# Moving the lower part of x to GpSimd and keeping the normalised x in PSUM

## The chip, the cores and the metric

One core of a Trainium2 chip. A core has TensorE (PE, matrix products, with a weight-load half PEld), VectorE (DVE), ScalarE (ACT), GpSimd (POOL) and SyncE (SP, which issues the transfers here). They run side by side and wait for each other through semaphores; matrix products land in PSUM, which has eight banks of 512 fp32 columns; all else is in SBUF. The metric is device time in microseconds of one execution, the median over runs.

## The reference

The input x is 16 sequences of 128 tokens with 128 features. It goes through one gated cross-attention, and then through six layers of local attention and feed-forward:

```python
x = x + tanh(g_xattn) * xattn(layernorm(x), ctx)
h = layernorm(x)
for i in range(6):
    h = attn_layer(shift_tokens(h), Wqkv[i], ...) + h   # 16 heads, windows of 32, rotary, l2norm
    h = ffn_layer(shift_tokens(h), g[i], b[i], W1[i], ...) + h
x = x + tanh(g_ffn) * h
```

`ffn_layer` normalises its input by feature, xn = (x - mean) / sqrt(var + 1e-5) * g + b, multiplies it by W1 (128 x 682), gates one half with the gelu of the other, and multiplies by W2.

## The kernel before

After a prologue for the cross-attention (some 75 us) the kernel runs 6 layers x 8 pairs of sequences = 48 pairs through a software pipeline. Each engine has its own loop over pairs with a body `step`, written out by hand, in which each call names its lag: `chunk(1, 0, 0)` on PE is product 1 of this turn's pair, sequence 0; `up(1, 2)` belongs to the pair of two turns before. The order of the calls is the order of the engine's queue, so an instruction that waits holds up all that follow it on its engine. GpSimd's loop is one turn behind the others: its `lag` of 1 or 2 stands for the pair that DVE calls with 0 or 1.

Products that need more precision than one pass split their operands in an upper and a lower part: x into `xsh` (ACT, `x_parts`, L538) and `xsl` = x - `xsh` (DVE, `x_rest`, L780), and the weights likewise into `Wh` and `Wl` (GpSimd, L384). A `product` is three matmuls, L1003 to L1005. The first product of a turn is `chunk(1, 0, 0)`, the second `chunk(0, 0, 0)`. Each waits for `xs_split` (xsl is there) and then for those who empty its bank: the first for earlier readers of a chunk, the second for ACT's copy `v_out(0, 1, 1)` (L576).

The normalisation for the feed-forward goes: PE `centre` puts the centred x into bank 3, ACT `deviations` squares it, PE `variance` averages, ACT `inverse_deviation` makes `rstdx` (L608, L611), DVE `normal` makes `xng` = centred x * g * `rstdx` in SBUF (L841), ACT `upper_x` adds b and rounds to `xfh` (L618), DVE `lower_x` makes `xfl` = xng + b - xfh (L849), and PE's `up` multiplies both parts by W1.

GpSimd adds the two halves of the rotary (`add`, L393), multiplies by the inverse norms (`normalise`, L407), divides by row sums (`divide`, L413) and makes `Wl`. Bank order is a table, `BANK_USERS`; `FREED` names who releases a bank after each kind of use. Bank 3's user after "xc" is `v_chunk(0, 0, 0)`.

Of the kernel before, what the change touches and what calls it, by code (L numbers as in the profile page):

```python
# [5 lines left out]
L, NB, S, D = 6, 16, 128, 128  # L6
# [25 lines left out]
def program(nc, x, ctxT, Wqkv, Wo, W1, W2, by_feature, every_token, shape_consts, out):  # L32
# [5 lines left out]
    def sb(name, shape, dt=F32):  # L38
        return es.enter_context(nc.sbuf_tensor(name, shape, dt))
# [4 lines left out]
    with es:  # L44
# [16 lines left out]
        F_LNG = 2 * 128 + 3  # L61
# [29 lines left out]
        sqx = sb("sqx", [128, 2 * S])  # L91
        lvx = sb("lvx", [128, 2 * S])
        rstdx = sb("rstdx", [128, 2 * S])
        xng = sb("xng", [128, 2 * S])
        xfh = sb("xfh", [128, 2 * S], F32R)
        xfl = sb("xfl", [128, 2 * S], F32R)
        gate = sb("gate", [128, KT2, 2 * S])
# [31 lines left out]
        def sems(name, n):  # L129
# [12 lines left out]
        res_done, xs_split, xng_done, xf_ready, hh_ready, h_ready = (  # L142
            sem(s) for s in ("res_done", "xs_split", "xng_done", "xf_ready", "hh_ready", "h_ready"))
        DVE_SEMS = (rot_done + ss_done + t2_done + mx_done + sc_out + sum_done + rs_done
                    + [res_done, xs_split, xng_done, xf_ready, hh_ready, h_ready])

        sq_done, v_ready, q_ready, k_ready = sems("sq_done", 4), sems("v_ready", 2), sems("q_ready", 2), sems("k_ready", 2)
        exp_done, PT_ready, OT_ready = sems("exp_done", 2), sems("PT_ready", 2), sems("OT_ready", 2)
# [5 lines left out]

        add_done, qk_ready, P_ready = sems("add_done", 4), sems("qk_ready", 4), sems("P_ready", 2)
        ss_ready, W_split = sem("ss_ready"), sem("W_split")
        POOL_SEMS = add_done + qk_ready + P_ready + [ss_ready, W_split]

        x_read = (ch_full[2], v_full[0])
        xf_read = up_full[2]  # L160
# [12 lines left out]
        def n_(n):  # L173
            return n + START

        def pipeline(eng, step, split_lag=0):
# [11 lines left out]
            for it in range(PAIRS, PAIRS + LAST):  # L188
# [7 lines left out]
                 "turn_p": lambda k: [PT_ready[k]],  # L196
                 "values": lambda k: [OT_ready[k]],
                 "Wo": lambda k: [res_done],
                 "xc": lambda k: [xng_done],
                 "up": lambda k: [[gelu_done], [hh_ready], [hh_ready]][k],  # L200
                 "down": lambda k: [h_ready]}
        BANK_USERS = [
# [47 lines left out]
        def column(at, pair, per=1, k=0, rows=slice(0, 128)):  # L250
            return fc[rows, ds(pair // LAYER_PAIRS * per + (at + k), 1)]
# [6 lines left out]

        def halves_of_pair(pair):
            return [R[64 * g:64 * g + 64, ds(pair % LAYER_PAIRS * 2, 2), g:g + S] for g in range(2)]  # L260

        def two(ap):
            return ap.rearrange("p (r s) -> p r s", r=2)
# [111 lines left out]
        @block.gpsimd  # L375
        def _(pool):
            for s in POOL_SEMS:
                pool.sem_inc(s, START)

            def lower_part(k, block):  # L380

                pool.wait_ge(high_ready, k + 1 + START)
                pool.sem_inc(wait_met, 1)
                nc.gpsimd.tensor_tensor(part_block(Wl, k, block), raw_block(block), part_block(Wh, k, block),  # L384
                                        ALU.subtract).then_inc(W_split, 1)

            def step(it, on, splitting):

                def add(c, lag, r):
                    n = (it - lag) * 2 + r  # L390
                    pool.wait_ge(rot_done[c], n_(n) + 1)
                    pool.wait_ge(t2_done[c], n_(n) + 1)
                    nc.gpsimd.tensor_tensor(u[:, r, c], u[:, r, c], t2[:, r, c % 2], ALU.add).then_inc(add_done[c], 1)  # L393

                def bound_norms(lag, r):
                    n = (it - lag) * 2 + r
                    for c in range(NCH):
                        pool.wait_ge(ss_done[c], n_(n) + 1)
                    pool.wait_ge(ln_done, n_(n) - 1)
                    pool.sem_inc(wait_met, 1)  # L400
                    nc.gpsimd.tensor_scalar_max(ssc[:, r], ss[:, r], 1e-24).then_inc(ss_ready, 1)

                def normalise(c, lag, r):
                    n = (it - lag) * 2 + r
                    pool.wait_ge(rn_ready, n_(n) + 1)
                    pool.wait_ge(add_done[c], n_(n) + 1)
                    nc.gpsimd.tensor_tensor(by_head(u[:, r, c]), by_head(u[:, r, c]),  # L407
                                            spread(rn[:, r, HC * c:HC * c + HC], HC, DH), ALU.mult).then_inc(qk_ready[c], 1)

                def divide(e, lag, r):  # L410
                    n = (it - lag) * 2 + r
                    pool.wait_ge(rs_done[e], n_(n) + 1)
                    nc.gpsimd.tensor_tensor(P[:, r, e], P[:, r, e], spread(rs[:, r, e], 8, DH),  # L413
                                            ALU.mult).then_inc(P_ready[e], 1)

                def split_low():
                    pair = it - LOW_LAG
                    lower_part(pair + LAYER_PAIRS, pair % LAYER_PAIRS)

                if on(2):  # L420
                    normalise(0, 2, 1)
                    add(2, 2, 1)
                    add(1, 2, 1)
                    normalise(2, 2, 1)
                    normalise(1, 2, 1)
                    divide(0, 2, 0)
                    divide(1, 2, 0)
                if on(1):
                    add(1, 1, 0)
                    add(0, 1, 0)  # L430
                if splitting:
                    split_low()
                if on(2):
                    divide(1, 2, 1)
                    divide(0, 2, 1)
                if on(1):
                    add(2, 1, 0)
                    bound_norms(1, 0)
                    normalise(2, 1, 0)
                    normalise(1, 1, 0)  # L440
                    add(3, 1, 0)
                    normalise(0, 1, 0)
                    normalise(3, 1, 0)
                    add(3, 1, 1)
                    bound_norms(1, 1)
                    add(0, 1, 1)
                    normalise(3, 1, 1)

            pool.wait_ge(in_ready, 16 * N_INPUTS)
            pool.sem_inc(c_ctx, START)  # L450
            with pool.Fori(0, NB // PAIR) as pair:
                pool.wait_ge(rest_ready, pair * 32 + START)
                for j in range(2):
                    g = pair * 2 + j
                    pool.wait_ge(c_v, g - 1 + START)
                    pool.sem_inc(wait_met, 1)
                    nc.gpsimd.tensor_copy(cT[j], ctxS[:, ds(g * GB, GB)].rearrange("p b d -> p (b d)")).then_inc(c_ctx, 1)
                for i in range(4):
                    lower_part(pair * 4 + i, pair * 4 + i)

            for w in range(2):
                nc.gpsimd.tensor_tensor(TC[:, :, w], qs[:, w], rc[:, w].unsqueeze(1).broadcast_to([128, L, DH]), ALU.mult)
                for a in range(2):
                    o, i = 32 * a, 32 * (1 - a)
                    nc.gpsimd.tensor_tensor(TS[:, :, w, o:o + 32], qs[:, w, :, i:i + 32],
                                            rsn[:, w, o:o + 32].unsqueeze(1).broadcast_to([128, L, 32]),
                                            ALU.mult).then_inc(tables_ready, 1)
            pool.wait_ge(tables_ready, 4)
            pipeline(pool, step, LOW_LAG)

        @block.scalar
        def _(act):
# [57 lines left out]
            def step(it, on, splitting):  # L530
# [82 lines left out]
                def upper_x(lag):  # L613
                    pair = it - lag
                    act.wait_ge(xng_done, n_(pair) + 1)
                    act.wait_ge(xf_read, n_(pair))
                    act.sem_inc(wait_met, 1)
                    nc.scalar.activation(xfh[:], xng[:], ACT.Identity, bias=column(F_LNB, pair)).then_inc(xfh_done, 1)  # L618

                def gelu(lag):  # L620
                    pair = it - lag
# [83 lines left out]
        def _(dve):  # L705
# [67 lines left out]

            def step(it, on, splitting):

                def x_rest(lag):
                    pair = it - lag
                    dve.wait_ge(xsh_ready, n_(pair) + 1)
                    dve.sem_inc(wait_met, 1)
                    nc.vector.tensor_tensor(xsl[:], shifted_pair(pair), xsh[:], ALU.subtract).then_inc(xs_split, 1)  # L780

                def squares(c, lag, r):
                    n = (it - lag) * 2 + r
                    dve.wait_ge(sq_done[c], n_(n) + 1)
# [51 lines left out]
                def normal(lag):  # L836
                    pair = it - lag
                    dve.wait_ge(rstd_ready, n_(pair) + 1)
                    dve.wait_ge(xfh_done, n_(pair))
                    dve.sem_inc(wait_met, 1)  # L840
                    nc.vector.scalar_tensor_tensor(out=xng[:], in0=bank_of("xc")[:, 0:2 * S], scalar=column(F_LNG, pair),  # L841
                                                   in1=rstdx[:], op0=ALU.mult, op1=ALU.mult).then_inc(xng_done, 1)

                def lower_x(lag):
                    pair = it - lag
                    dve.wait_ge(xfh_done, n_(pair) + 1)
                    dve.wait_ge(xng_done, n_(pair) + 1)
                    dve.sem_inc(wait_met, 1)
                    nc.vector.scalar_tensor_tensor(out=xfl[:], in0=xng[:], scalar=column(F_LNB, pair), in1=xfh[:],  # L849
                                                   op0=ALU.add, op1=ALU.subtract).then_inc(xf_ready, 1)  # L850

                def gated(lag):
# [25 lines left out]
                if on(1):  # L878
                    straight(2, 1, 1)
                    swapped(1, 1, 1)  # L880
                    swapped(2, 1, 1)
                if on(0):
                    x_rest(0)
                if on(2):
                    normal(2)
                if on(1):
# [387 lines left out]
```

## Time and profile before

| | |
|---|---|
| median of 3 runs | 1595.66 us (1594.83 to 1598.72) |
| profiled execution, its time / its span | 1600.49 / 1598.6 us |
| busy, share of the span | PE 94%, PEld 78%, DVE 88%, ACT 74%, POOL 73% |
| mean granted PE clock | 0.976 of full |
| xsl L780 on DVE | 48 x 1341 ns mean |
| xng L841 / xfl L849 on DVE | 48 x 472 / 917 ns mean |
| xfh L618 on ACT | 48 x 510 ns mean |

A row of the time line has the start (us from the span's start), the busy time of the group in us, engine, line, operation, the tiles written and read, and the count; in brackets the engine's idle time before it and who ended it. A row of the table of waits has the waiting engine and line, whom it waited for, and the total, the number and the longest of these waits in us.

### The profile page before, as it was taken

The page shows a single profiled execution, that of the slowest core. Times are in us where ns is not written, and L with a number is a line of the kernel's source. Part 1 is how long each engine was busy: PE and PEld are TensorE (multiplying, and loading weights), DVE is VectorE, ACT ScalarE, POOL GpSimd, SP SyncE. Part 2 cuts the span into 40 slices and gives each one's busy share as a digit, 9 for nine tenths or more (in the row PEclk, how much of TensorE's full clock was granted, in tenths as well). Part 3 has the DMA queues.
Part 4 walks back from the last instruction along what each step waited for, and adds up shares of the span by engine and source line. Part 5 has one row for each costly group of instructions (what it writes and reads, how often), then busy time and mean ns, then how long its engine had stood idle before and what let it go on. Part 6 is the DMA issues. An engine that isn't in the chain of part 4 may idle for free.

```text
span 1598.6 us, 80227 instructions
## 1 busy us (share of the span) xinstructions
PE 1506.6 (94%) x31136; PEld 1251.0 (78%) x31136; DVE 1399.6 (88%) x2545; ACT 1175.3 (74%) x2333; POOL 1168.4 (73%) x1118
## 2 busy tenths in 40 slices
PE   4589999999999999999999999999999999999996
PEld 3367888888888888888888888888888888888875
DVE  3587899999999999989999999999999999999982
ACT  3456687788778778778877877877877777777772
POOL 1276777878877887787787788788778777777760
PEclk8689999999999999999999999999999999999996
DMA  5110011011110111101112110111110101000010
GB/s 144 42 44 28 28 36 42 26 49 58 31 36 26 42 39 57 41 26 36 42 29 68 29 38 29 33 42 61 36 35 20 30 25 62 29 20 30 20 30 28
DMA packets 41462, 62.40 MB, mean 39 GB/s; under 512 B 3662, under 2 KB 30412, under 8 KB 41420
## 3 DMA queue, kind: packets, MB, share of 16 engines
q1 hardware_dynamic: 41420, 61.84, 13.2%
q8 instruction: 27, 0.44, 0.1%
q14 instruction: 15, 0.12, 0.0%
HBM read 18.84 MB, written 1.05 MB: 12 GB/s over the span
## 4 chain that ended last, share of the span: by engine, by line
PE 86%; issue 4%; ACT 3%; DVE 2%; ACTq 1%; POOL 0%; DVEq 0%; POOLq 0%
PE bank L1010 13%; PE bank L1080 12%; PE bank L1092 10%; PE bank L1003 9%; PE bank L1053 8%; PE bank L1004 8%; PE bank L1005 8%; PE bank L1127 5%; PE bank L1116 3%; PE bank L1035 3%; PE bank L1117 2%; PE bank L1118 2%; ACT v L576 2%; DVE xng L841 1%; PE bank L1106 1%
## 5 line engine op out<-in xcount | busy, mean ns | idle before, releaser
L393 POOL TENSOR_TENSOR u<-u,t 128x512 f32<-128x512 f32 x384 | 498.2, 1308 | 40.5 <-DVE t L802 40.5
L407 POOL TENSOR_TENSOR u<-u,rn 128x512 f32<-128x512 f32 x384 | 401.8, 1068 | 78.8 <-ACT rn L556 78.8
L413 POOL TENSOR_TENSOR P<-P,rs 128x512 f32<-128x512 f32 x192 | 196.5, 1045 | 172.6 <-DVE rs L826 172.6
L1003 PE MATMUL bank<-Wl,xsh 128*128 (+1 forms) x576 | 273.4, 475 | 26.1 <-ACT v L576 22.7
L802 DVE TENSOR_TENSOR t<-bank,TS 128x512 f32<-128x512 f32 x384 | 258.0, 682 | 28.1 <-ACT sq L545 25.5
L793 DVE TENSOR_TENSOR u<-bank,TC 128x512 f32<-128x512 f32 x384 | 261.9, 682 | 6.0 <-ACT sq L545 3.1
L786 DVE TENSOR_REDUCE ss<-sq 128x8 f32<-128x512 f32 x384 | 250.5, 673 | 6.4 <-ACT sq L545 6.4
L1004 PE MATMUL bank<-Wh,xsl 128*128 (+1 forms) x576 | 228.5, 397 | 0.0
L1005 PE MATMUL bank<-Wh,xsh 128*128 (+1 forms) x576 | 228.0, 396 | 0.0
L545 ACT ACTIVATE sq<-bank 128x512 f32<-128x512 f32 x384 | 218.9, 598 | 5.8 <-PE bank L1005 5.3
L1010 PE MATMUL bank<-shape_constants,u 128*128 128x128 f32 x1536 | 219.2, 275 | 3.4 <-POOL u L407 3.2
L1010 PEld LDWEIGHTS bank<-shape_constants,u 128*128 128x128 f32 x1536 | 182.2, 141 | 34.9 <-POOL u L407 5.0
L562 ACT COPY qT<-bank 128x512 f32<-128x512 f32 x192 | 115.2, 600 | 122.3 <-PE bank L1010 121.1
L1080 PEld LDWEIGHTS bank<-PT,vs 64*64 64x64 f32 x6144 | 163.9, 135 | 37.5 <-issue 37.5
L1080 PE MATMUL bank<-PT,vs 64*64 64x32 f32 x6144 | 187.8, 220 | 3.0 <-ACT PT L588 3.0
L1080 PE MATMUL bank<-PT,v 64*64 64x32 f32 x6144 | 186.1, 219 | 2.6 <-issue 2.6
L1092 PE MATMUL bank<-OT,WoS 128*128 128x256 f32 x768 | 175.5, 382 | 1.2 <-ACT OT L594 1.2
L1080 PEld LDWEIGHTS bank<-PT,v 64*64 64x64 f32 x6144 | 164.7, 135 | 2.8 <-issue 2.8
L1003 PEld LDWEIGHTS bank<-Wl,xsh 128*128 128x128 f32 x576 | 109.5, 190 | 62.5 <-issue 55.7
L1092 PEld LDWEIGHTS bank<-OT,WoS 128*128 128x128 f32 x768 | 143.4, 192 | 19.2 <-issue 1.3
L1053 PEld LDWEIGHTS bank<-kT,qT 64*32 64x32 f32 x12288 | 123.3, 105 | 32.3 <-issue 32.3
L594 ACT COPY OT<-bank 128x512 f32<-128x512 f32 x192 | 109.1, 594 | 45.4 <-PE bank L1080 45.4
(102 smaller groups left out, 3040.0 us busy)
## 6 DMA issues: line engine op xcount, KB each, us to landing
vs<-v SPq DMA_DIRECT2D x96, 384.0 KB, 3.3
Wraw<-in_L_ffn_Wqkv_dram SPq DMA_DIRECT2D x72, 117.5 KB, 2.1
WoS<-in_L_ffn_Wo_dram SPq DMA_DIRECT2D x6, 512.0 KB, 3.7
W1h<-Wh SPq DMA_DIRECT2D x6, 341.0 KB, 2.5
W1l<-Wl SPq DMA_DIRECT2D x6, 341.0 KB, 2.9
Wraw<-in_L_ffn_W_dram SPq DMA_DIRECT2D x12, 116.0 KB, 2.2
OT<-in_x_dram SPq DMA_DIRECT2D x2, 512.0 KB, 5.6
v<-in_ctx_dram SPq DMA_DIRECT2D x2, 512.0 KB, 6.9
```

The costliest lines, as they stand in the source:

```text
L393: nc.gpsimd.tensor_tensor(u[:, r, c], u[:, r, c], t2[:, r, c % 2], ALU.add).then_inc(add_done[c], 1)
L407: nc.gpsimd.tensor_tensor(by_head(u[:, r, c]), by_head(u[:, r, c]), spread(rn[:, r, HC * c:HC * c + HC], HC, DH), ALU.mult).then_inc(qk_re ...
L786: nc.vector.tensor_reduce(ss[:, r, HC * c:HC * c + HC], by_head(square_out(c, r)), AX, ALU.add).then_inc(ss_done[c], 1)
L793: nc.vector.tensor_tensor(by_head(u[:, r, c]), by_head(bank_of("chunk", c, r)[:]), TC[:, layer(it - lag), c % 2].broadcast_to([128, HC, DH ...
L802: nc.vector.tensor_tensor(halves(t2[:, r, c % 2]), halves(bank_of("chunk", c, r)[:])[:, :, ::-1, :], TS[:, layer(it - lag), c % 2].broadca ...
L1003: nc.tensor.matmul(out, x[0], Wl[:, w], start=True, stop=False)
L1004: nc.tensor.matmul(out, x[1], Wh[:, w], start=False, stop=False)
L1005: nc.tensor.matmul(out, x[0], Wh[:, w], start=False, stop=True).then_inc(done, 1)
L1010: i = nc.tensor.transpose(bank[:, 128 * t:128 * t + 128], src[:, 128 * t:128 * t + 128], ident[:])
L1053: i = nc.tensor.matmul(bank_of("scores", e, r)[64 * w2 + 32 * a:64 * w2 + 32 * a + 32, at + (32 if w == 0 else 0):at + 64], qT[f, s, t, 32 ...
L1080: i = nc.tensor.matmul(bank_of("values", h, r)[64 * e:64 * e + 64, 64 * t + 32 * w2:64 * t + 32 * w2 + 32], (vs, v)[w2][p, r, head:head + ...
L1092: i = nc.tensor.matmul(bank_of("Wo")[:, 0:2 * S], WoS[:, k], OT[:, k].rearrange("p r s -> p (r s)"), start=(k == 0), stop=(k == INNER // 1 ...
```

## The change

The subtraction that makes `xsl` moves from DVE's queue, where it stood between `swapped(2, 1, 1)` and `normal(2)`, to GpSimd's, where it stands between `add(2, 2, 1)` and `add(1, 2, 1)`. The tile `xng` goes: `normal` writes its result over the centred x in bank 3, and `upper_x` and `lower_x` read it from there. The bank is now released by `xf_ready` (after `lower_x`) in place of `xng_done`.

```diff
-        xng = sb("xng", [128, 2 * S])
...
-                 "xc": lambda k: [xng_done],
+                 "xc": lambda k: [xf_ready],
...
+        def normal_bank():
+            return bank_of("xc")[:, 0:2 * S]
...  GpSimd
+                def x_rest(lag):
+                    pair = it - lag
+                    pool.wait_ge(xsh_ready, n_(pair) + 1)
+                    pool.sem_inc(wait_met, 1)
+                    nc.gpsimd.tensor_tensor(xsl[:], shifted_pair(pair), xsh[:], ALU.subtract).then_inc(xs_split, 1)
...
                     add(2, 2, 1)
+                if on(1):
+                    x_rest(1)
+                if on(2):
                     add(1, 2, 1)
...  ScalarE, upper_x
-                    nc.scalar.activation(xfh[:], xng[:], ACT.Identity, bias=column(F_LNB, pair)).then_inc(xfh_done, 1)
+                    nc.scalar.activation(xfh[:], normal_bank(), ACT.Identity, bias=column(F_LNB, pair)).then_inc(xfh_done, 1)
...  VectorE, normal and lower_x
-                    nc.vector.scalar_tensor_tensor(out=xng[:], in0=bank_of("xc")[:, 0:2 * S], scalar=column(F_LNG, pair),
+                    nc.vector.scalar_tensor_tensor(out=normal_bank(), in0=normal_bank(), scalar=column(F_LNG, pair),
                                                    in1=rstdx[:], op0=ALU.mult, op1=ALU.mult).then_inc(xng_done, 1)
...
-                    nc.vector.scalar_tensor_tensor(out=xfl[:], in0=xng[:], scalar=column(F_LNB, pair), in1=xfh[:],
+                    nc.vector.scalar_tensor_tensor(out=xfl[:], in0=normal_bank(), scalar=column(F_LNB, pair), in1=xfh[:],
...
-                if on(0):
-                    x_rest(0)
                 if on(2):
                     normal(2)
```

DVE's queue near the start of the loop's body, before (L802 is `swapped`, L810 `maxima`, L817 `minus_maxima`; REGISTER_ALU and ISA rows work out addresses and waits):

```order
L802 TENSOR_TENSOR t2<-bank_6,TS 128x512
L778 REGISTER_ALU
L780 ISA
L780 TENSOR_TENSOR xsl<-R,xsh 128x256
L839 REGISTER_ALU
L841 ISA
L841 SCALAR_TENSOR_TENSOR xng<-bank_3,feature_columns,rstdx 128x256
L808 REGISTER_ALU
L810 TENSOR_REDUCE nm<-bank_7 128x8
L810 TENSOR_REDUCE nm<-bank_5 128x8
L849 ISA
L849 SCALAR_TENSOR_TENSOR xfl<-xng,feature_columns,xfh 128x256
```

The same place of DVE's queue now (line numbers are those of the changed kernel; L807 is `swapped`, L815 `maxima`):

```order
L807 TENSOR_TENSOR t2<-bank_6,TS 128x512
L844 REGISTER_ALU
L846 ISA
L846 SCALAR_TENSOR_TENSOR bank_3<-bank_3,feature_columns,rstdx 128x256
L813 REGISTER_ALU
L815 TENSOR_REDUCE nm<-bank_7 128x8
L815 TENSOR_REDUCE nm<-bank_5 128x8
L854 ISA
L854 SCALAR_TENSOR_TENSOR xfl<-bank_3,feature_columns,xfh 128x256
```

The subtraction is gone from between `swapped` and `normal`; the rest stands in the same order, with bank 3 in place of `xng`.

GpSimd's queue at the start of the loop's body, before:

```order
L407 TENSOR_TENSOR u<-u,rn 128x512
L393 TENSOR_TENSOR u<-u,t2 128x512 x2
L407 TENSOR_TENSOR u<-u,rn 128x512 x2
L412 REGISTER_ALU
L413 TENSOR_TENSOR P<-P,rs 128x512 x2
```

And now (L415 is `normalise`, L401 `add`, L421 `divide`, L395 the subtraction):

```order
L415 TENSOR_TENSOR u<-u,rn 128x512
L401 TENSOR_TENSOR u<-u,t2 128x512
L393 REGISTER_ALU
L395 ISA
L395 TENSOR_TENSOR xsl<-R,xsh 128x256
L401 TENSOR_TENSOR u<-u,t2 128x512
L415 TENSOR_TENSOR u<-u,rn 128x512 x2
L420 REGISTER_ALU
L421 TENSOR_TENSOR P<-P,rs 128x512 x2
```

One subtraction of 256 columns stands between the two adds; everything behind it on GpSimd keeps its order.

## Rows read from the trace of the kernel before

**Rows 1.** Busy time by stretch, middle of the span: length, then each engine's.

```profile
800.00:1000.00 200.00, 196.50 (x4174) 164.01 (x4167) 184.71 (x323) 154.43 (x306) 160.17 (x152) 1.00 0.13 40
```

**Rows 2.** Table of waits, whole span: total us, times, longest.

```profile
PEld bank L1003 <- issue: 55.7, 87, 3.1
...
ACT xfh L618 <- DVE xng L841: 48.0, 48, 1.0
...
PE bank L1003 <- ACT v L576: 22.7, 46, 1.3
```

**Rows 3.** Time line of PE, one turn of the loop.

```profile
812.58 0.48 PE L1003 MATMUL bank<-Wl,xsh 128*128 x1
812.89 0.40 PE L1004 MATMUL bank<-Wh,xsl 128*128 x1
813.12 0.39 PE L1005 MATMUL bank<-Wh,xsh 128*128 x1
814.01 0.50 PE L1003 MATMUL bank<-Wl,xsh 128*128 x1 [0.50 <-ACT v L576]
...
816.91 0.60 PE L1010 MATMUL bank<-shape_constants,u 128*128 128x128 f32 x4
```

**Rows 4.** Time line of ACT, the same turn.

```profile
810.00 0.40 ACT L538 CAST xsh<-R 128x256 fp32r x1 [0.54 <-PE bank L1005]
...
810.86 0.42 ACT L611 ACTIVATE rstdx<-lvx 128x256 f32<-128x256 f32 x1
...
812.78 0.51 ACT L618 ACTIVATE xfh<-xng,feature_columns 128x256 fp32r<-128x256 f32 x1 [1.03 <-DVE xng L841]
813.20 0.56 ACT L576 COPY v<-bank 128x512 f32<-128x512 f32 x1
```

**Rows 5.** Time line of DVE, the same turn.

```profile
810.73 1.38 DVE L780 TENSOR_TENSOR xsl<-R,xsh 128x256 fp32r<-128x256 f32 x1 [0.78 <-ACT xsh L538]
812.03 0.47 DVE L841 SCALAR_TENSOR_TENSOR xng<-bank,feature_columns,rstdx 128x256 f32<-128x256 f32 x1
```

**Rows 6.** Groups of instructions by line: duration in ns, min/median/max; lvx busy, mean.

```profile
L780 DVE TENSOR_TENSOR xsl<-R,xsh x48: 425/1379/1522, 78.0 to 1515.5; 128x256 fp32r<-128x256 f32 x48
...
L849 DVE SCALAR_TENSOR_TENSOR xfl<-xng,feature_columns,xfh x48: 485/910/1345, 132.7 to 1577.4; 128x256 fp32r<-128x256 f32 x48
...
L393 POOL TENSOR_TENSOR u<-u,t x384: 1266/1288/1490, 82.4 to 1547.1; 128x512 f32<-128x512 f32 x192
...
L384 POOL TENSOR_TENSOR Wl<-Wraw,Wh x48: 1175/1190/1226, 22.8 to 1284.1; - x38, 128x470 f32 x8, 128x470 fp32r<-128x470 f32 x2
...
L465 POOL TENSOR_TENSOR TS<-every_token_rows,shape_constants x4: 526/528/528, 57.9 to 60.2; 128x192 f32<-128x192 f32 x4
...
L608 ACT ACTIVATE lvx<-bank,cols 128x256 f32<-128x256 f32 x48 | 22.8, 474 | 1.8 <-PE bank L1106 1.8
```

**Rows 7.** Time line of POOL, the same turn; the first add once alone.

```profile
810.54 1.28 POOL L393 TENSOR_TENSOR u<-u,t 128x512 f32<-128x512 f32 x1
...
808.54 2.05 POOL L407 TENSOR_TENSOR u<-u,rn 128x512 f32<-128x512 f32 x2 [0.52 <-ACT rn L556]
810.54 2.70 POOL L393 TENSOR_TENSOR u<-u,t 128x512 f32<-128x512 f32 x2
813.21 2.22 POOL L407 TENSOR_TENSOR u<-u,rn 128x512 f32<-128x512 f32 x2
818.63 2.05 POOL L413 TENSOR_TENSOR P<-P,rs 128x512 f32<-128x512 f32 x2 [3.20 <-DVE rs L826]
```

**Rows 8.** Time line of an early turn, before the loop's body proper.

```profile
130.00 0.43 DVE L780 TENSOR_TENSOR xsl<-R,xsh 128x256 fp32r<-128x256 f32 x1 [0.73 <-ACT xsh L538]
...
130.39 0.42 ACT L611 ACTIVATE rstdx<-lvx 128x256 f32<-128x256 f32 x1
...
130.99 0.48 DVE L841 SCALAR_TENSOR_TENSOR xng<-bank,feature_columns,rstdx 128x256 f32<-128x256 f32 x1 [0.56 <-ACT rstdx L611]
...
132.98 0.40 PE L1003 MATMUL bank<-Wl,xsh 128*128 128x512 f32 x1
```

More of the change, by code:

```diff
@@ L144, in program @@
         DVE_SEMS = (rot_done + ss_done + t2_done + mx_done + sc_out + sum_done + rs_done
-                    + [res_done, xs_split, xng_done, xf_ready, hh_ready, h_ready])
+                    + [res_done, xng_done, xf_ready, hh_ready, h_ready])
         sq_done, v_ready, q_ready, k_ready = sems("sq_done", 4), sems("v_ready", 2), sems("q_ready", 2), sems("k_ready", 2)
@@ L156, in program @@
         ss_ready, W_split = sem("ss_ready"), sem("W_split")
-        POOL_SEMS = add_done + qk_ready + P_ready + [ss_ready, W_split]
+        POOL_SEMS = add_done + qk_ready + P_ready + [ss_ready, W_split, xs_split]
         x_read = (ch_full[2], v_full[0])
@@ L774, in step @@
             def step(it, on, splitting):
[L776 to L780, printed above, removed]
                 def squares(c, lag, r):
```

## The prediction

> **What bounds the kernel now.** I read three views: busy time by stretch, the table of waits, and the time line of one turn of the loop. The stretch in the middle [rows 1] has TensorE (PE) busy 196.50 of 200 us at full clock, VectorE (DVE) 184.71, GpSimd (POOL) 160.17, ScalarE (ACT) 154.43. So the loop runs at PE's pace, and an edit is worth only what it takes out of, or adds to, PE's waits. The table of waits [rows 2] has one that comes once a pair: L1003, the first matmul of a product, waits for ACT's copy of v (L576) 46 times, 22.7 us; the weight loads of the same line stand idle 55.7 us, and 48.0 us stand against ACT's xfh (L618), which waits for DVE's xng (L841) in every pair.
>
> The time line puts these in one place. PE starts the three matmuls of chunk(1, 0, 0) at 812.58, 812.89 and 813.12 [rows 3]: steps of 0.31 and 0.23, so the next product could start at 813.12 + 0.23 = 813.35. It starts at 814.01: 0.66 us lost in a turn (the table counts 0.50, since it lets a matmul's modelled end run on). That product, chunk(0, 0, 0), needs the bank that v_out(0, 1, 1) empties. On ACT [rows 4] that copy starts at 813.20, right behind xfh, which starts at 812.78 after 1.03 us of idling for DVE. On DVE [rows 5] xng starts at 812.03, though its input rstdx was there at 810.86 + 0.42 = 811.28 [rows 4]: DVE was in xsl, the subtraction L780, from 810.73 to 812.11. So the chain into PE's one steady stall is xsl, xng, xfh, v, PE.
>
> xsl is long because it runs beside GpSimd. Its 256 columns take 0.425 us at the least and 1.379 in the median [rows 6]. The long ones fit GpSimd's add, which runs from 810.54 to 811.82 [rows 7]: 0.29 us behind its end xsl ends too. In an early turn, at 130.00, xsl took 0.43 [rows 8]; xng then began at 130.99, 0.18 behind rstdx, and PE's second product followed at 132.98 with no wait marked. That turn shows, unasked, what the stall hangs on.
>
> **The change, part by part.**
>
> *xsl leaves DVE.* xng can now start when rstdx is done plus the hand-over from ACT to DVE. In the loop that hand-over is 810.73 - (810.00 + 0.40) = 0.33 us, from xsh to xsl [rows 4, 5]. So xng runs 811.61 to 812.08, in place of 812.03 to 812.50. The hand-over to ACT stays 812.78 - 812.50 = 0.28: xfh starts at 812.36. ACT is free by then: its 1.03 us of idling began at 811.75 [rows 4].
>
> *xng is made in PSUM, and xfh and xfl are made from there.* No row shows DVE writing PSUM. Below, it is 0.47, as now; above, the 0.91 of the two-operand xfl beside GpSimd [rows 6]. I take 0.47: that instruction already reads the bank. xfh's nearest row with a bias and a source in PSUM is lvx, 0.474 [rows 6], against 0.51 now, so it is 0.04 shorter. v_out starts 0.42 behind xfh now (813.20 - 812.78), then 0.38: 812.74; it takes 0.56 and its hand-over to PE is 814.01 - 813.76 = 0.25 [rows 3, 4]. By this path PE's chunk(0, 0, 0) could start at 813.55. xfl has one operand in SBUF less and falls from 0.91 to the 0.485 of its fastest row [rows 6]; it lies behind that stall, and up(1, 2), which needs it, comes only after chunk(0, 0, 0), so I count it at nothing. What hides it is that product on PE. xfl ends 0.42 earlier with xng and 0.42 more by itself, 0.84, and PE comes 0.4 sooner: nothing gets late there. The bank is released later (after xfl, not after xng), but the next writer of it, v_chunk(0, 0, 0), stands on PE behind up(1, 2), which waits for xfl anyhow: no cost.
>
> The Trainium skill speaks against this part: Perfetto Trace Analysis, "Optimizing Scalar/DVE Operations", gives a DVE instruction some 60 ns of access overhead in SBUF and some 125 in PSUM, and a ScalarE one 93 and 51. By it xng would be 0.065 longer and xfh 0.042 shorter, which makes this path 0.02 us later than with neither. That xng from PSUM to SBUF takes 0.47 and xfl from SBUF alone 0.485 at best does not show such a gap, so the sum goes without it.
>
> *xsl goes to GpSimd.* Its queue gets 48 instructions more, between add(2, 2, 1) and add(1, 2, 1). What an instruction of 256 columns costs there no row shows. GpSimd takes 1.288 for 512 columns (L393) and 1.190 for 470 (L384), both with two whole operands and a result of the same width [rows 6]: 0.0023 us a column, so about 0.69 for 256. The bounds are 0.53, which 192 columns take with one operand repeated (L465), and 1.29, the whole 512. I take 0.69. It cannot start before the add ends at 811.82 (810.54 + 1.28 [rows 7]); xsh is there since 810.40. So xsl is ready at 812.51, where it was ready at 812.11. PE was at chunk(1, 0, 0) at 812.58, so the slack was 0.47 and is now 0.07, before any hand-over. Behind the wait for xsl PE still has the waits for that bank, so I take the longest hand-over of these rows, 0.33, with 0.25 and twice 0.33 as bounds. chunk(1, 0, 0) then starts at 812.84, 0.26 late, and ends its three steps (813.35 - 812.58 = 0.77) at 813.61. This is past the 813.55 of the other path, so GpSimd now sets PE's start: 813.61 in place of 814.01, a gain of 0.40 us a pair.
>
> What queues behind it on GpSimd: add(1, 2, 1) and two multiplications, L407, that ended at 813.21 + 2.22 = 815.43 [rows 7]. They come 0.69 later, less what DVE's two colliding instructions cost GpSimd: the pair of adds took 2.70 and the pair of multiplications 2.22, where two alone take 2 x 1.28 and 2.05 [rows 7]; that is 0.14 and 0.17 back. So they end at 815.81. PE's turn_qk(1, 1, 1) needs the last; it stood at 816.91 [rows 3] and will be at 816.51: 0.70 of room, 0.37 with a hand-over of 0.33. Then GpSimd has idled 3.20 us before L413 [rows 7], and the delay ends there.
>
> What follows the stall starts from PE's products or from xfh, and both come about 0.4 earlier. I find no further wait that the 0.40 would run into.
>
> **Sum.** 46 x 0.40 = 18.4 us. The profiled execution took 1600.49 (span 1598.6), so 1582.1; the median before, 1595.66, is 0.997 of that execution, and the same share gives 1577.3.
>
> **Rivals.**
>
> *The whole stall goes.* If GpSimd's subtract comes near 0.53 and both hand-overs near what the turn at 130 shows (0.18 from rstdx to xng [rows 8]), both paths are in time: 46 x 0.66 = 30.4, that is 1565.3. For it: that turn of the loop has no stall. Against: it ran outside the loop proper, where less address arithmetic stands before an instruction, and with xsl ready early.
>
> *No change.* xng gets slow as it is written to PSUM, or what comes out of xng's earlier start is given back as a later chunk(1, 0, 0): with xsl ready plus hand-over at 813.24 the start of chunk(0, 0, 0) is where it was. That is reached with xng at 0.94, or with 0.69 + 0.73 on GpSimd's path: 1595.7. For it: no row has either operation. Against: both are twice their nearest rows.
>
> *Slower.* GpSimd's subtract costs as much as a whole add, 1.29, because it is paced by something else than columns. xsl is then ready at 813.11, PE starts chunk(1, 0, 0) at 813.44 and chunk(0, 0, 0) at 814.21: 0.20 lost in each of 46 turns, 9.2 us, 1604.9. It decides from 1.09 us on (811.82 + 1.09 + 0.33 + 0.77 = 814.01). From there the multiplications behind it also come near turn_qk. For it: PE's slack to xsl was only 0.47 and this path now carries the bound. Against: the 192-column rows at 0.53 [rows 6] say that GpSimd is paced by columns.
>
> **How the numbers follow.** Forecast, with its own bounds: 0.07 (hand-over 0.66) to 0.46 (the other path's limit) a pair, 3 to 21 us, 1574 to 1592: 0.70. Whole stall gone: 0.09. No change: 0.10. Slower: 0.09. The rest, 0.02, is larger losses. A change under 0.3%, 4.8 us, cannot be told from none. Faster: 0.67 of the forecast, the whole-stall case 0.09, and 0.04 of "no change", 0.80. Same: 0.03 and 0.05, 0.08. Slower: the rest, 0.12. The range reaches from the whole-stall case to the bound of 0.07: 1566 to 1594.
>
> **What the profile after would show.** xsl as a GpSimd row of about 0.7 us between two adds of 1.28; xng about 0.3 behind rstdx, 0.4 earlier against PE's first chunk; xfh's wait for xng down from about 1.0 to 0.6 a pair; xfl near 0.48; the pairs of L393 and L407 at 2.56 and 2.05; L1003's wait for ACT v mostly gone, with a smaller wait of L1003 for xsl in its place. Wrong: xsl over 1 us on GpSimd, a wait of L1010 for L407, or a new steady wait of PE elsewhere.

## The result, and the profile after

The changed kernel takes 1574.18 us (median of 4 runs, 1572.64 to 1575.57), the kernel before 1596.22 on the same chip (4 runs, 1594.83 to 1598.72): a ratio of 0.986, 95% interval 0.9843 to 0.9877. That is 22.0 us gained where 18.4 were forecast (1577.3); the profiled execution took 1572.64, its span 1570.8. Every ratio below is to the kernel before, run beside it, with its 95% interval in brackets.

The table of waits over the whole span, total us, times, longest:

```profile
PEld bank L1006 <- issue: 34.6, 88, 3.4
...
ACT xfh L629 <- DVE bank L846: 32.4, 48, 0.8
...
PE bank L1006 <- POOL xsl L395: 3.0, 1, 3.0
```

Against [rows 2] the weight loads of chunk (L1003, now L1006) stand idle 34.6 us and not 55.7; xfh waits 0.68 a pair (32.4 / 48) and not 1.00; PE's 46 waits for ACT's v are gone from the list but for one of 1.3 us. PE waits for xsl on GpSimd once.

Where this arises is read in one turn. ACT's xsh is the turn's zero: 810.00 before [rows 4], 824.88 after, so 14.88 is taken off each time below to compare it with one of before. ACT, then DVE, then GpSimd, then PE (start, us, instruction, idle time before it):

```profile
824.88 0.40 ACT L549 CAST xsh<-R 128x256 fp32r x1 [0.54 <-PE bank L1008]
...
825.75 0.42 ACT L622 ACTIVATE rstdx<-lvx 128x256 f32<-128x256 f32 x1
...
827.32 0.47 ACT L629 ACTIVATE xfh<-bank,feature_columns 128x256 fp32r<-128x256 f32 x1 [0.69 <-DVE bank L846]
827.69 0.58 ACT L587 COPY v<-bank 128x512 f32<-128x512 f32 x1
```

```profile
826.55 0.49 DVE L846 SCALAR_TENSOR_TENSOR bank<-bank,feature_columns,rstdx 128x256 f32<-128x256 f32 x1 [1.70 <-ACT rstdx L622]
...
828.14 0.48 DVE L854 SCALAR_TENSOR_TENSOR xfl<-bank,feature_columns,xfh 128x256 fp32r<-128x256 f32 x1
```

```profile
825.45 1.27 POOL L401 TENSOR_TENSOR u<-u,t 128x512 f32<-128x512 f32 x1
826.68 0.64 POOL L395 TENSOR_TENSOR xsl<-R,xsh 128x256 fp32r<-128x256 f32 x1
827.27 1.29 POOL L401 TENSOR_TENSOR u<-u,t 128x512 f32<-128x512 f32 x1
```

```profile
827.51 0.49 PE L1006 MATMUL bank<-Wl,xsh 128*128 x1
...
828.07 0.40 PE L1008 MATMUL bank<-Wh,xsh 128*128 x1
828.52 0.49 PE L1006 MATMUL bank<-Wl,xsh 128*128 x1
...
829.31 0.28 PE L1119 MATMUL bank<-xfh,W1l 128*85 128x256 f32 x1
829.43 0.28 PE L1120 MATMUL bank<-xfl,W1h 128*85 128x256 f32 x1
```

DVE is idle when rstdx ends at 826.17, and the normalisation starts at 826.55; taken back by 14.88 that is 811.67, where it was 812.03 [rows 5]. xfh comes at 812.44 (was 812.78), v at 812.81 (was 813.20), chunk(1, 0, 0) at 812.63 (was 812.58: 0.05 late) and chunk(0, 0, 0) at 813.64 (was 814.01 [rows 3]): 0.37 gained there. PE's last step of chunk(1) begins at 828.07; 0.23 later, at 828.30, the next product could run; it starts at 828.52. So 0.22 us a turn of the stall is left, and the wait for it is still v: the copy ends at 827.69 + 0.58 = 828.27, and 0.25 more, the hand-over of [rows 3, 4], is 828.52. (A hand-over is the time from the end of one engine's instruction to the start of the one that waited for it.)

Over many turns: from xsh at 411.61 to xsh at 1269.69 lie 28 turns of the kernel before, 30.646 us each; from 402.20 to 1277.72 lie 29 of the changed one, 30.190 each (the two first rows are of before, in a fence of their own):

```profile
411.61 0.41 ACT L538 CAST xsh<-R 128x256 fp32r x1 [0.54 <-PE bank L1005]
1269.69 0.40 ACT L538 CAST xsh<-R 128x256 fp32r x1 [0.54 <-PE bank L1005]
```

```profile
402.20 0.40 ACT L549 CAST xsh<-R 128x256 fp32r x1 [0.53 <-PE bank L1008]
1277.72 0.40 ACT L549 CAST xsh<-R 128x256 fp32r x1 [0.54 <-PE bank L1008]
```

That is 0.456 a turn, and 46 x 0.456 = 21.0 of the 22.0 us. "A turn" means this difference from here on; for the experiments it is worked out in the same way.

Durations over the span, ns, min/median/max:

```profile
L395 POOL TENSOR_TENSOR xsl<-R,xsh x48: 629/688/740, 76.3 to 1489.6; 128x256 fp32r<-128x256 f32 x48
...
L846 DVE SCALAR_TENSOR_TENSOR bank<-bank,feature_columns,rstdx x48: 492/493/494, 130.5 to 1548.0; 128x256 f32<-128x256 f32 x48
...
L854 DVE SCALAR_TENSOR_TENSOR xfl<-bank,feature_columns,xfh x48: 475/476/483, 132.2 to 1549.2; 128x256 fp32r<-128x256 f32 x48
...
L401 POOL TENSOR_TENSOR u<-u,t x384: 1262/1283/1314, 80.9 to 1519.6; 128x512 f32<-128x512 f32 x192
```

xsl on GpSimd has the 0.69 that was taken for it, in the median: its turns alternate between 0.64 and 0.73. xfl no longer spreads (485/910/1345 in [rows 6], now 475 to 483), and GpSimd's adds take 1314 at most, not 1490: in this profile neither side is held by the other any more.

### The profile page after: what moved, and what is told of

It is laid out like the page before. It is cut to its first block, busy times and chain, and to the rows that moved or that the text cites. A ratio compares the mean times of both kernels' runs of the same rounds, so it can differ in the third digit from the quotient of the medians.

```text
span 1570.8 us, 80227 instructions
## 1 busy us (share of the span) xinstructions
PE 1502.9 (96%) x31136; PEld 1254.1 (80%) x31136; DVE 1317.8 (84%) x2497; ACT 1167.1 (74%) x2333; POOL 1180.8 (75%) x1166
## 4 chain that ended last, share of the span: by engine, by line
PE 92%; issue 1%; ACT 1%; DVE 1%; POOL 0%; ACTq 0%; DVEq 0%; POOLq 0%
PE bank L1013 16%; PE bank L1083 12%; PE bank L1095 11%; PE bank L1006 10%; PE bank L1007 8%; PE bank L1008 8%; PE bank L1056 8%; PE bank L1130 5%; PE bank L1119 3%; PE bank L1038 3%; PE bank L1120 2%; PE bank L1121 2%; PE bank L1109 1%; PE bank L1103 1%; PE bank L1209 0%
## 5 line engine op out<-in xcount | busy, mean ns | idle before, releaser
L401 POOL TENSOR_TENSOR u<-u,t 128x512 f32<-128x512 f32 x384 | 490.7, 1283 | 23.9 <-DVE t L807 23.9
L415 POOL TENSOR_TENSOR u<-u,rn 128x512 f32<-128x512 f32 x384 | 393.0, 1045 | 75.9 <-ACT rn L567 75.9
L421 POOL TENSOR_TENSOR P<-P,rs 128x512 f32<-128x512 f32 x192 | 196.3, 1043 | 124.0 <-DVE rs L831 124.0
L807 DVE TENSOR_TENSOR t<-bank,TS 128x512 f32<-128x512 f32 x384 | 258.8, 684 | 29.2 <-ACT sq L556 26.6
L1006 PE MATMUL bank<-Wl,xsh 128*128 (+1 forms) x576 | 273.3, 475 | 5.8 <-POOL xsl L395 3.0
L815 DVE TENSOR_REDUCE nm<-bank 128x8 f32<-128x512 f32 x192 | 127.3, 684 | 20.0 <-PE bank L1056 20.0
L1006 PEld LDWEIGHTS bank<-Wl,xsh 128*128 128x128 f32 x576 | 109.2, 190 | 43.7 <-issue 34.6
```

The costliest lines, as they stand in the source:

```text
L807: nc.vector.tensor_tensor(halves(t2[:, r, c % 2]), halves(bank_of("chunk", c, r)[:])[:, :, ::-1, :], TS[:, layer(it - lag), c % 2].broadca ...
L1006: nc.tensor.matmul(out, x[0], Wl[:, w], start=True, stop=False)
```

## The experiments

Two theories stood against each other. **Collision:** xsl is long only because GpSimd reads beside it, and the gain is xsl's disappearance from ahead of the normalisation. **Bank:** the gain comes from the x kept in PSUM (shorter xfh and xfl).

**The change in two halves.** First only xsl moves, with xng left in SBUF:

```
...  VectorE's x_rest goes, GpSimd gets one, at the place shown above
-                    nc.vector.tensor_tensor(xsl[:], shifted_pair(pair), xsh[:], ALU.subtract).then_inc(xs_split, 1)
+                    nc.gpsimd.tensor_tensor(xsl[:], shifted_pair(pair), xsh[:], ALU.subtract).then_inc(xs_split, 1)
...
```

> Only the subtraction for xsl moves to GpSimd; the normalised x stays in its SBUF tile. My theory: the gain is xng starting behind rstdx instead of behind xsl, so this half gives nearly all of it: chunk(0, 0, 0) 0.35 to 0.40 us earlier a turn, 16 to 20 us in all, ratio to the kernel before 0.987 to 0.990. xfl still runs beside GpSimd and stays near 0.9 us. Rival: keeping the normalised x in PSUM carries half of the gain or more (shorter xfh, shorter xfl, GpSimd undisturbed); then this half gives 8 to 11 us, ratio 0.993 to 0.995.

Measured: 1575.50 us, ratio 0.9863 [0.9844, 0.9882], a turn 0.418 shorter. That is all of the change, within the interval. In the turn whose xsh starts at 827.00, PE has:

```profile
830.66 0.49 PE L1004 MATMUL bank<-Wl,xsh 128*128 x1
...
831.58 0.28 PE L1118 MATMUL bank<-xfl,W1h 128*85 128x256 f32 x1
```

chunk(0, 0, 0) starts 3.66 behind xsh, where it was 814.01 - 810.00 = 4.01: 0.35 gained, as expected. xfl did not stay near 0.9: it takes 0.736 in the median, 0.70 in this turn. Then only the other half, xsl left on DVE:

```
-                    ... scalar_tensor_tensor(out=xng[:], in0=bank_of("xc")[:, 0:2 * S], ...
+                    ... scalar_tensor_tensor(out=normal_bank(), in0=normal_bank(), ...
...  upper_x, lower_x and the release of the bank as in the change
```

> Only the normalised x stays in PSUM; xsl is still made by DVE. My theory: xng still starts behind xsl, so chunk(0, 0, 0) gains at most 0.02 us; up(1, 2), which in the kernel before started 0.03 to 0.06 us late because xfl ended at 814.53, gains that: 1 to 4 us in all, ratio 0.997 to 1.000, with xfl near 0.48 us. Rival: DVE has 0.44 us less to do in each of 48 turns and GpSimd is slowed once less, and this is what the time follows: 10 us or more, ratio under 0.994.

Measured: 1591.17, ratio 0.9956 [0.9938, 0.9973], a turn 0.083 shorter. The stall stays where it was, in PE's time line (810.55 - 809.69 - 0.23 = 0.63 us, before 0.66):

```profile
809.69 0.40 PE L1007 MATMUL bank<-Wh,xsh 128*128 x1
810.55 0.49 PE L1005 MATMUL bank<-Wl,xsh 128*128 x1 [0.46 <-ACT v L578]
...
811.35 0.28 PE L1118 MATMUL bank<-xfh,W1l 128*85 128x256 f32 x1
811.47 0.28 PE L1119 MATMUL bank<-xfl,W1h 128*85 128x256 f32 x1
```

But up(1, 2), the product behind it, is no longer held. Its first two matmuls are 0.12 apart here and 0.16 in the kernel before, 814.83 and 814.99:

```profile
814.83 0.32 PE L1116 MATMUL bank<-xfh,W1l 128*85 128x256 f32 x1
814.99 0.28 PE L1117 MATMUL bank<-xfl,W1h 128*85 128x256 f32 x1
```

The waits of before have a line for it that I had passed over, 45 idle times of that product's weight loads, and this run's list has none such:

```profile
PEld bank L1116 <- issue: 13.1, 45, 0.4
```

The line names nobody; that the wait was for xfl follows from the two halves: in both xfl is ready earlier, and the line is gone here and down to 8 waits, 1.8 us, with xsl moved. So the bank half is worth a little by itself, through a second wait behind the first. 46 x 0.083 = 3.8 of the 7.2 us; where the other 3 come from is not located. DVE has 0.44 us a turn less to do here (xfl takes 0.470 in the median and not 0.910), so its load is not what the time follows.

**Is it the collision, or GpSimd taking the work?** xsl stays on DVE, and GpSimd's add only waits until it is done, in the kernel before. (The run with one operand, which the text below names, was made before this one and is told next.)

```
                 if on(2):
                     normalise(0, 2, 1)
+                    if on(1):
+                        pool.wait_ge(xs_split, n_(it - 1) + 1)
                     add(2, 2, 1)
```

> The kernel before, with one wait more: GpSimd starts add(2, 2, 1) only when DVE has made xsl. Nothing moves to another engine and no operand changes; GpSimd is only not reading while xsl is made. My theory: xsl then takes 0.43 us in every turn, xng starts 0.3 to 0.4 behind rstdx, and chunk(0, 0, 0) is 0.35 to 0.40 earlier, as with xsl on GpSimd: ratio 0.986 to 0.990. xfl stays near 0.9. GpSimd's adds start 0.7 us late, and turn_qk still has room for that. Rival, left open by the run with one operand: xsl is long because of its place or its rows; then it stays at 1.38 and GpSimd is late as well, ratio 1.000 or above.

Measured: 1577.04, ratio 0.9885 [0.9864, 0.9907], a turn 0.407 shorter. DVE's time line:

```profile
826.12 0.42 DVE L782 TENSOR_TENSOR xsl<-R,xsh 128x256 fp32r<-128x256 f32 x1 [0.80 <-ACT xsh L540]
827.07 0.48 DVE L843 SCALAR_TENSOR_TENSOR xng<-bank,feature_columns,rstdx 128x256 f32<-128x256 f32 x1 [0.53 <-ACT rstdx L613]
```

The same subtraction on the same engine takes 0.42 in place of 1.38 [rows 5] (0.425 in the median over the span), and nearly the whole gain is there without moving it. So xsl was long for the add beside it, not for its place or its rows. xfl came out shorter than expected here too (0.766 in the median).

**Which operand collides.** xsl becomes an instruction with one tile and two columns of constants. This kernel leaves xsh out of the subtraction.

```
-                    nc.vector.tensor_tensor(xsl[:], shifted_pair(pair), xsh[:], ALU.subtract).then_inc(xs_split, 1)
+                    nc.vector.tensor_scalar(xsl[:], shifted_pair(pair), fc[:, F_B2:F_B2 + 1], fc[:, F_B2:F_B2 + 1],
+                                            ALU.subtract, ALU.mult).then_inc(xs_split, 1)
```

> The kernel before, with DVE's instruction for xsl still there, on the same 256 columns and at the same place, but with one tile as operand: it takes x minus a column of constants times a column, and leaves out xsh, so the lower part of x is not the real one. My theory: xsl is long because it reads two tiles of SBUF while GpSimd reads there; with one it takes 0.33 to 0.50 us, xng starts 0.3 to 0.4 us behind rstdx, and the gain is that of moving xsl to GpSimd, 0.37 to 0.40 a turn, ratio 0.987 to 0.990, though DVE gave nothing away. xfl stays near 0.9. Rival: xsl is long for the place it stands in (its operand from ACT has just been written, or the strided rows of R); then it stays near 1.3 and the ratio is 1.000.

Measured: 1590.10, ratio 0.9954 [0.9937, 0.9971], a turn 0.134 shorter. My form of the theory, "two tiles in SBUF", fell: with one tile it is held too. DVE (one turn, then all over the span), then GpSimd:

```profile
803.87 1.25 DVE L780 TENSOR_SCALAR xsl<-R,feature_columns 128x256 fp32r x1 [0.79 <-ACT xsh L538]
```

```profile
L780 DVE TENSOR_SCALAR xsl<-R,feature_columns x48: 412/1245/1499, 77.8 to 1505.6; 128x256 fp32r x45, 128x256 fp32r<-128x256 f32 x3
```

```profile
803.68 2.56 POOL L393 TENSOR_TENSOR u<-u,t 128x512 f32<-128x512 f32 x2
```

It is 0.13 us shorter in the median than [rows 6], as the turn is, and it ends at 805.12. The first of the two adds ends near 803.68 + 2.56 / 2 = 804.96, so DVE is done 0.16 behind it and not 0.29. By the Trainium skill, SBUF — State Buffer, "Who interferes with whom", DVE shares one pair of ports with GpSimd; an instruction with two inputs in SBUF meets GpSimd's reads there, one with at most one input does not unless it enters a 2-port mode, as tensor_scalar can, and whoever comes first holds the pair for its whole instruction. In the loop's turns the runs agree with the last point (xsl ends just behind the add, and takes 0.42 with no add beside it), and with xfl, which from the bank and one tile takes 475 to 483 ns; that it was a 2-port mode here, no run shows. One early turn of this run does not fit who comes first, if the starts tell it: xsl starts at 129.62, the add at 129.70, and xsl takes 1.50 all the same. That the two columns of constants count as a second input was not tried.

**Two chains, two waits.** ACT has xfh and then v_out(0, 1, 1) in its queue. If v goes first, chunk(0, 0, 0) needs nothing of DVE:

```
+                if on(1):
+                    v_out(0, 1, 1)
                 if on(2):
                     upper_x(2)
                 if on(1):
-                    v_out(0, 1, 1)
                     queries(0, 1, 1)
```

In the kernel before:

> The kernel before, with the same two calls on ACT exchanged and nothing else. My theory: chunk(0, 0, 0) no longer stalls (0.66 us earlier), but up(1, 2) right behind it still needs xfl, which ended at 814.53 and is not earlier, so PE stalls there instead, before L1116: 0 to 5 us gained, ratio 0.997 to 1.000. Rival: the stall was only that copy's place in ACT's queue, and up has room; then all 0.66 a turn goes, 30 us, ratio 0.981, and moving xsl was not needed.

Measured: 1597.95, ratio 0.9997 [0.9984, 1.0009]. The stall at chunk is gone, and all of it stands at the next product, which waits for xfl in every turn (time line, then the table of waits):

```profile
812.20 0.40 PE L1004 MATMUL bank<-Wl,xsh 128*128 x1
...
812.67 0.39 PE L1006 MATMUL bank<-Wh,xsh 128*128 x1
813.67 0.32 PE L1117 MATMUL bank<-xfh,W1l 128*85 128x256 f32 x1 [0.61 <-DVE xfl L850]
```

```profile
PE bank L1117 <- DVE xfl L850: 32.9, 48, 3.1
```

In the changed kernel:

> The changed kernel, with ACT's v_out(0, 1, 1) put ahead of upper_x, so that the copy that PE waits for no longer stands behind xfh. My theory: what is left of the stall at chunk(0, 0, 0), 0.22 us a turn, is still this chain and goes: 8 to 11 us less than the changed kernel, ratio to the kernel before 0.979 to 0.981. xfh does not get later, since it waits for xng. Rival 1: xsl on GpSimd is what sets the pace now; then nothing changes (0.986). Rival 2: up(1, 2) becomes the wait because xfl is not ready; then under half, 0.983 to 0.986.

Measured: 1561.11, ratio 0.9767 [0.9749, 0.9785], a turn 0.729 shorter than before. Both products follow without a gap, at steps of 0.23:

```profile
824.89 0.40 PE L1009 MATMUL bank<-Wh,xsh 128*128 x1
825.13 0.40 PE L1007 MATMUL bank<-Wl,xsh 128*128 x1
...
825.83 0.28 PE L1120 MATMUL bank<-xfh,W1l 128*85 128x256 f32 x1
```

A gap also makes the first step behind it longer (828.85 - 828.52 = 0.33 in the changed kernel, 0.23 here), so this turn of 29.86 us is 0.32 shorter than one of the changed kernel, and not 0.22. But every other turn takes some 29.98. In those GpSimd's subtraction takes 0.73 and not 0.64, and PE's chunk(1, 0, 0) starts 0.19 behind its end:

```profile
853.37 0.73 POOL L395 TENSOR_TENSOR xsl<-R,xsh 128x256 fp32r<-128x256 f32 x1
```

```profile
854.29 0.50 PE L1007 MATMUL bank<-Wl,xsh 128*128 x1
```

In the turns of 29.86 it does so too (824.33, behind 823.50 + 0.64). So with v first the first rival has a part: how long GpSimd takes for xsl is now passed on to the whole turn.

The same swap with one half of the change each, first the bank half:

> xsl still on DVE; the normalised x in PSUM; and on ACT v_out(0, 1, 1) ahead of upper_x. My theory: two chains end at about the same point of PE's queue, one over xfh and v into chunk(0, 0, 0), one over xfl into up(1, 2). With v first only the second is left, and the PSUM half shortens it by the 0.43 us that xfl loses: up(1, 2) at 813.26 in place of 813.67, 0.41 a turn, 18 us, ratio 0.987 to 0.990, where the two edits alone gave 0.9956 and 0.9997. Rival: the edits just add up, 0.995; then the two chains are not what hides one edit behind the other.

Measured: 1575.73, ratio 0.9869 [0.9846, 0.9891]. So the bank half is worth 7 us alone and some 20 behind the swap ((0.9997 - 0.9869) x 1597), which is worth nothing alone. With the GpSimd half:

> xsl on GpSimd, the normalised x in SBUF as before, and on ACT v_out(0, 1, 1) ahead of upper_x. My theory: chunk(0, 0, 0) loses its stall, and xfl, 0.70 us beside GpSimd, is now 0.15 us late for up(1, 2): ratio 0.980 to 0.983, between the GpSimd half alone (0.9863) and the changed kernel with the same exchange (0.9767). Rival 1: the same 0.977, so the PSUM half is worth nothing in any company. Rival 2: no gain over 0.986.

Measured: 1575.64, ratio 0.9874 [0.9853, 0.9896]. The turn is 0.531 shorter than before, 0.113 shorter than with that half alone, as chunk(0, 0, 0) no longer stalls; xfl, 0.71 here, makes up(1, 2) late. But the total did not move from the 0.9863 of that half, so 46 x 0.113 = 5 us are missing outside these turns. In the two profiled executions they lie at the ends: from the first xsh to the sixth 146.16 us against 144.13, behind the last xsh 83.51 against 80.64. Over the profiles of the other kernels that last stretch lies between 80.7 and 85.0; why it differs stays open.

**What GpSimd's path can bear.** A second, unused subtraction ahead of xsl's in the changed kernel:

```
+                    nc.gpsimd.tensor_tensor(spare[:], shifted_pair(pair), xsh[:], ALU.subtract)
                     nc.gpsimd.tensor_tensor(xsl[:], shifted_pair(pair), xsh[:], ALU.subtract).then_inc(xs_split, 1)
```

> The changed kernel, with GpSimd doing the subtraction twice: first into a spare tile, then into xsl. This gives xsl the 1.3 us that my case on the slower side supposed. My theory: PE's first chunk then waits for GpSimd; xsl would end at 827.92 in place of 827.32 in the turn read of the changed kernel, chunk(1, 0, 0) start at 828.11 and chunk(0, 0, 0) at 828.90 in place of 828.52: 0.38 us a turn, up to 0.55 in turns where the subtraction takes 0.73, 17 to 25 us lost against the changed kernel, ratio to the kernel before 0.997 to 1.002. Rival: GpSimd's queue has room, as its waits of 2 us before L421 say; then the time stays at 0.986.

Measured: 1590.45, ratio 0.9967 [0.9952, 0.9982], a turn 0.361 longer than after, 46 x 0.361 = 16.6 us. PE now waits for xsl in each turn; GpSimd first, then PE (the time line, and its row in the table of waits), then ACT:

```profile
807.95 0.73 POOL L396 TENSOR_TENSOR spare<-R,xsh 128x256 fp32r<-128x256 f32 x1
808.64 0.72 POOL L397 TENSOR_TENSOR xsl<-R,xsh 128x256 fp32r<-128x256 f32 x1
```

```profile
809.55 0.49 PE L1008 MATMUL bank<-Wl,xsh 128*128 x1 [0.54 <-POOL xsl L397]
...
810.34 0.39 PE L1008 MATMUL bank<-Wl,xsh 128*128 x1
...
811.03 0.28 PE L1121 MATMUL bank<-xfh,W1l 128*85 128x256 f32 x1
```

```profile
PE bank L1008 <- POOL xsl L397: 23.6, 46, 3.7
```

```profile
806.18 0.40 ACT L551 CAST xsh<-R 128x256 fp32r x1 [0.53 <-PE bank L1010]
```

xsl ends at 809.36, and PE starts at 809.55: the hand-over is 0.19. Counted from xsh, chunk(0, 0, 0) starts at 4.16 (before 4.01), but up(1, 2) right behind it at 4.85 (before 814.83 - 810.00 = 4.83). So two subtractions only bring such a turn back to about where it was (30.61 us, before 30.65); the turns in between, with 0.64 and 0.65, take 30.46.

**A placement question.** The 48 subtractions on GpSimd alternate between 0.64 and 0.73 by the turn. In this kernel R's rows are padded from S + 1 to S + 4 columns, the rest is the changed kernel:

> The changed kernel, with rows of R of 132 columns in place of 129, so that a pair of rows is 1056 bytes and not 1032. In the changed kernel the subtraction on GpSimd alternates between 0.64 and 0.73 us from pair to pair. If the start of the operand in its row is the cause (1032 bytes a pair shift it by 8 in every 16), all of them take 0.64 now. If it is what runs beside it on other engines, the alternation stays. In both cases the time stays within 0.3% of the changed kernel, since the first chunk is not what PE waits longest for there.

Measured: 1570.91 us, where the changed kernel has 1572.64 to 1575.57; one run decides nothing on the time.

```profile
L395 POOL TENSOR_TENSOR xsl<-R,xsh x48: 722/734/748, 76.9 to 1489.6; 128x256 fp32r<-128x256 f32 x48
```

The alternation is gone, so it hung on where the operand starts. But all are at 0.73 and none at the 0.64 that I expected; why, with the distance between the rows changed as well, stays open.

**A version that beats both.** GpSimd's wait, the bank half and v first, with xsl on DVE:

> The same wait on GpSimd, with the normalised x in PSUM and v_out(0, 1, 1) ahead of upper_x; xsl stays on DVE. My theory: what counts is that xng starts right behind rstdx and that xfl is short, on whichever engine xsl is made; so this comes to the time of the changed kernel with v first, ratio 0.976 to 0.979. Rival: GpSimd's late adds make turn_qk(1, 1, 1) wait, or DVE, fuller by 0.4 us a turn, becomes a bound; then 0.980 or more.

Measured: 1560.91, ratio 0.9773 [0.9751, 0.9796], as good as the changed kernel with v first: in the time, moving xsl to GpSimd and keeping GpSimd out of its way come to the same. By the turn, 0.787 shorter than before, this kernel is 0.058 ahead, since none of its turns waits for a GpSimd subtraction of 0.73. PE in the middle stretch (length, then busy time of PE, weight loads, DVE, ACT, GpSimd), here and in the changed kernel:

```profile
800.00:1000.00 200.00, 200.00 (x4335) 169.45 (x4335) 182.08 (x337) 159.16 (x314) 160.60 (x156) 1.00 0.14 41
```

```profile
800.00:1000.00 200.00, 199.82 (x4329) 167.72 (x4328) 177.82 (x328) 159.01 (x314) 160.51 (x158) 1.00 0.14 42
```

The two differ by 0.18 in 200 us, yet their turns by 0.331 in 30. A matmul is drawn past the start of the next (0.40 at steps of 0.23), and longer behind a gap (0.49 in the rows above), so PE's busy time hides the rest of the stall. The starts show it.

## Why the prediction was right

*Place and cause.* That xsl, stretched by GpSimd's add, sits in the chain into PE's steady stall was right: the first half alone, and the wait on GpSimd alone, each give nearly the whole gain, and have no other edit in common.

*xng earlier.* Forecast 811.61, measured 811.67; the hand-over from ACT was 0.38 and not 0.33. xfh was forecast at 812.36 and v at 812.74; they came at 812.44 and 812.81.

*PSUM.* DVE writes the bank in 0.493, where 0.47 was taken; xfh is 0.474, as its nearest row said. Most of the 0.02 is not PSUM's. Behind a wait, xng takes 484 ns into SBUF too, as the first half alone shows (busy us and mean ns, then the idle time before):

```profile
L844 DVE SCALAR_TENSOR_TENSOR xng<-bank,feature_columns,rstdx 128x256 f32<-128x256 f32 x48 | 23.2, 484 | 83.8 <-ACT rstdx L620 83.8
```

Right behind xsl it takes 481 into PSUM in the bank half, and 472 into SBUF in the kernel before. So PSUM as the place written costs 0.009 either way. By an estimate from the Trainium skill's overheads (Perfetto Trace Analysis, "Optimizing Scalar/DVE Operations") xng would have been 0.065 longer and xfh 0.042 shorter; the rows give 0.009 and 0.036.

*GpSimd sets the pace.* This step failed. Its cost was right (0.69), but its hand-over to PE was sized at 0.33 and is 0.19 in the run with two subtractions. So chunk(1, 0, 0) comes 0.05 late and not 0.26 in the turn read, where the subtraction takes 0.64, and 0.12 late where it takes 0.73. In the turn read it would let chunk(0, 0, 0) start at 828.30, which is 813.42 in the times of before. The other path, forecast at 813.55, ended at 813.64, and this is PE's start. That the forecast 813.61 was nearly hit all the same (0.37 gained and not 0.40) is luck: the two paths lie that near. The smaller wait of PE for xsl that the prediction looked for in the table stands there once, not in each turn. GpSimd sets PE's start only where v goes first, or where it makes two subtractions.

*xfl counted at nothing.* This was mis-sized. Up(1, 2) did wait a little for it, 45 times, and its release adds 0.07: from the start of chunk(0, 0, 0) to the second matmul of up(1, 2) it was 814.99 - 814.01 = 0.98 and is 829.43 - 828.52 = 0.91. 0.37 + 0.07 = 0.44 of the 0.456 a turn. This, and not GpSimd, is why a turn gains more than 0.40; 1.0 of the 22.0 us lies outside the 46 turns. The bank is not needed for it: with xng still in SBUF the first half alone has 831.58 - 830.66 = 0.92, since xfl starts earlier and is held less.

*Queues behind.* GpSimd's adds came out as forecast (1.27 and 1.29), and PE's turn_qk waits for a multiplication only 3 times in the whole list, 3.3 us in all, so not in each turn.

*Rivals.* The whole stall does not go: 0.22 of 0.66 is left, and it takes ACT's order to remove it. The slower case was to decide at 1.09 us on GpSimd; with 0.73 + 0.72 there the kernel is still at 0.9967, since the hand-over is 0.14 shorter and up(1, 2) then follows chunk(0, 0, 0) without a gap (0.69 behind it, before 0.82); with the 0.69 that one costs, this case was far off.

## What to carry to other kernels

An instruction whose median is three times its shortest may be delayed and not expensive, as xsl was: look for what its neighbour engine runs until just before its end, and try an order in which they do not meet before moving the work. Where two chains end in neighbouring waits of the bounding engine, edits that are worth little or nothing alone can be worth much together (here 7 us and none alone, 21 together), so look behind the first wait for the second, also in the weight loads' lines. Read the bounding engine's starts, not its busy share.

## What the runs showed of the hardware that was not expected

A DVE tensor_scalar with one tile in SBUF was held by GpSimd's add as the two-tile subtraction was (1.245 us in the median, 0.412 at the least), but it cost the adds nothing: the pair took 2.56, beside the two-tile subtraction 2.70 [rows 7]. A GpSimd subtraction of 256 columns takes 0.64 or 0.73 us, from pair to pair, with rows of 129 columns, and 0.73 in all pairs with rows of 132. DVE writing in place into PSUM costs 0.009 us more than into SBUF; that it starts behind a wait and not right behind another instruction costs 0.012.
